# A graph layer with nearest neighbours: 48 quads of stage 1 multiplied as fp32r halves made by ScalarE and POOL

## The reference

```
z   = leaky_relu(lap(A, x) @ W1 + b1, 0.1)
S   = exp(-sqrt(|z_i - z_j|^2 + 1e-10) / 2), the 4 largest of each row kept
out = lap(S + A, x) @ W2 + b2
result = layernorm(x + out)
```

## Time and profile before

| | us |
|---|---|
| median of 3 runs | 2694.85 |
| lowest and highest run | 2694.80, 2696.83 |
| span of the profiled execution | 2759.5 |
| TensorE matmul busy in it | 2482.6 (90%) |
| DVE | 2319.8 (84%) |
| ScalarE | 1606.7 (58%) |
| POOL | 1195.4 (43%) |
| mean granted clock of TensorE | 0.969 |

### The profile page before, as it was taken

The page is one execution under the profiler, slowest core; times in us unless marked ns, Lnnn a source line. Parts: engine busy times, 40 slices in busy tenths (PEclk is TensorE's granted clock), DMA queues, the critical chain, the costliest instruction groups (busy, mean ns, idle before and its releaser), DMA issues.

```text
span 2759.5 us, 29107 instructions
## 1 busy us (share of the span) xinstructions
PE 2482.6 (90%) x9356; PEld 1722.4 (62%) x9356; DVE 2319.8 (84%) x1411; ACT 1606.7 (58%) x1905; POOL 1195.4 (43%) x987
## 2 busy tenths in 40 slices
PE   1367999999999998899999999999999987888978
PEld 0133444444677776578787877778787764666655
DVE  7998899977788888999999999999999773666766
ACT  0000000000477767999989899899988763555655
POOL 0000000000000000377778878788878956666760
PEclk9688999999999999999999999999999988999989
DMA  9999999995899960146555655555655688988975
GB/s 385 421 402 408 398 421 421 421 421 215 320 349 342 338 226 7 35 141 183 151 163 138 179 142 175 140 170 149 174 143 167 182 309 343 347 324 320 345 295 208
DMA packets 147949, 718.58 MB, mean 260 GB/s; under 512 B 19025, under 2 KB 26961, under 8 KB 86609
## 3 DMA queue, kind: packets, MB, share of 16 engines
q1 hardware_dynamic: 124384, 670.49, 65.6%
q0 software_dynamic: 18800, 37.77, 5.7%
q10 hardware_dynamic: 4608, 8.39, 0.8%
HBM read 680.40 MB, written 36.18 MB: 260 GB/s over the span
## 4 chain that ended last, share of the span: by engine, by line
PE 56%; issue 10%; ACT 10%; DVE 9%; DMA 7%; POOL 3%; another core or an unknown queue 3%; SPq 0%; ACTq 0%; POOLq 0%; DVEq 0%
PE PS L767 17%; PE PS L866 5%; PE PS L868 5%; PE PS L867 5%; DMA ring<-at 4%; ACT R L1141 3%; PE PS L834 3%; PE PS L910 3%; PE PS L921 3%; PE PS L911 3%; PE PS L830 2%; PE PS L831 2%; ACT ah_t L1191 2%; DVE R L1621 2%
## 5 line engine op out<-in xcount | busy, mean ns | idle before, releaser
L1299 POOL TENSOR_TENSOR al<-ring,ah 128x1024 fp32r<-128x1024 f32 x264 | 644.0, 2441 | 180.5 <-ACT ah L1112 168.7
L1621 DVE MAX8 R<-R 128x8 f32<-128x8192 f32 x64 | 555.9, 8685 | 68.1 <-ACT R L1141 67.9
L1141 ACT ACTIVATE R<-PS 128x1024 f32<-128x1024 f32 x512 | 518.1, 1018 | 114.1 <-PE PS L874 83.1
L1624 DVE FIND_INDEX8 R<-R,R 128x8 uint32<-128x8192 f32 x64 | 555.9, 8685 | 0.3 <-issue 0.3
L1272 POOL CAST zst<-zh 128x128 fp32r<-128x128 f32 (+1 forms) x64 | 26.2, 410 | 1113.2 <-DVE zl L1556 811.5
L866 PE MATMUL PS<-zh,zst 128*128 128x512 f32 x1024 | 407.3, 398 | 28.6 <-ACT PS L1127 12.7
L868 PE MATMUL PS<-zh,zst 128*128 128x512 f32 x1024 | 400.4, 391 | 0.0
L867 PE MATMUL PS<-zl,zst 128*128 128x512 f32 x1024 | 400.1, 391 | 0.0
L1456 POOL DMA_INDIRECT R<-xs_dram,R x256 | 279.7, 1093 | 145.2 <-issue 75.5
L1127 ACT ACTIVATE PS<-R 128x1024 f32<-128x1024 f32 x310 | 318.0, 1026 | 6.6
L1046 ACT ACTIVATE tiny<-rowsum 128x4 f32<-128x4 f32 x16 | 3.3, 205 | 481.2 <-DVE rowsum L1491 481.2
(11 more groups left out here) (177 smaller groups left out, 4469.9 us busy)
## 6 DMA issues: line engine op xcount, KB each, us to landing
R<-at SPq DMA_DIRECT2D x152, 1024.0 KB, 13.3
ring<-at SPq DMA_DIRECT2D x148, 1024.0 KB, 9.5
ring<-at SPq DMA_DIRECT2D x264, 512.0 KB, 3.9
cache<-at SPq DMA_DIRECT2D x117, 1024.0 KB, 20.2
raw_sq<-at SPq DMA_DIRECT2D x21, 1024.0 KB
raw_z<-at SPq DMA_DIRECT2D x20, 1024.0 KB
raw_ring<-at SPq DMA_DIRECT2D x20, 1024.0 KB
acc_dram<-R POOLq DMA_DIRECT2D x78, 256.0 KB, 5.7
```

The costliest lines, as they stand in the source:

```text
L1141: act.activation(score[j % 2][:, c * EC:(c + 1) * EC].rearrange("p (b c) -> p b c", b=2), pair(first, j, c), ACT.Copy).then_inc(copied, 1)
L1299: pool.tensor_tensor(al[:, k % SPLIT], raw[k % RAW], ah[:, k % SPLIT].bitcast(F32), ALU.subtract)\
L1621: v.max(top[:, j], score[j % 2]).then_inc(dve3, 1)
L1624: v.max_index(place[:, j], top[:, j], score[j % 2]).then_inc(placed, 1)
```

## The change

In row blocks 10 to 15 the eight quads with q < 8 are multiplied as halves: 48 quads. At the end of block 9 ScalarE makes the high halves of xs for q < 8 (two copies of 128x2048) and POOL the low ones. They lie in four slots of `cache`, which no load uses from load 144 on. Per halved quad ScalarE copies two pieces of 128x1024 to fp32r into one of two buffers, which lie over xs of q < 8; POOL subtracts each piece from the raw quad, with the result written over it, once DVE has added the quad; TensorE makes eight matmuls with the high part and four with the rest. Stage 2 writes its rests over the raw quads too, which frees two buffers for loads. In the order of loads and products of blocks 10 to 15 the halved quads are spread among the others.

```
-SLOTS_END = (0, 1, 2, 3, SLOTS_2, SLOTS_2 + B // TB)
+SLOTS_END = (0, 1, 2, 3, 4, 5)
+HALVED_FROM, HQ = 10, 8
+SLOTS_LOW = (SLOTS_2, SLOTS_2 + 1, SLOTS_2 + 4, SLOTS_2 + 5)
...
+def on_halves(b, q):
+    return b >= HALVED_FROM and q < HQ
...
+        if b == HALVED_FROM:
+            low = [HQ] + low[:HQ] + low[HQ + 1:]
+        elif b > HALVED_FROM:
+            low = spread(low[:HQ], low[HQ:-2]) + low[-2:]
...
-            k = next_slot(n, [*range(SLOTS_A), *(k for k, b in SLOTS_Y.items() if left(n) <= B * (b + 1)),
+            k = next_slot(n, [*(k for k in range(SLOTS_A) if n < (HALVED_FROM - 1) * B or k not in SLOTS_LOW),
+                              *(k for k, b in SLOTS_Y.items() if left(n) <= B * (b + 1)),
...
-            k = next_slot(n, [*range(SLOTS_B), *range(SLOTS_A, SLOTS_A + SLOTS_X)])
+            k = next_slot(n, [*range(SLOTS_2), *range(SLOTS_A, SLOTS_A + SLOTS_X)])
...
-        halves = range(min(q for r, q in two), B)
+        halves = range(HQ, B)
...
-                    sp.wait_ge(al_ok, m - n_one + 1)
+                    sp.wait_ge(prod2, m - n_one + 1)
...
+            def halved_product(b, q, first):
...
+                for k in range(TB):
+                    if k % PT == 0:
+                        pe.wait_ge(rnd_1, RESTS * m + k // PT + 1)
+                    pe.matmul(bank, half_of_xs(0, q)[:, k], ah_2[m % 2][:, k], start=first and k == 0, stop=False,
+                              skip_group_check=True)
+                    pe.matmul(bank, half_of_xs(1, q)[:, k], ah_2[m % 2][:, k], start=False, stop=False,
+                              skip_group_check=True)
+                for k in range(TB):
+                    if k % PT == 0:
+                        pe.wait_ge(al_1, RESTS * m + k // PT + 1)
+                    i = pe.matmul(bank, half_of_xs(0, q)[:, k], low[:, k], start=False, stop=False,
+                                  skip_group_check=True)
+                i.then_inc(prod1, 1)
...
+            def high_halves_low():
+                for k in range(2):
+                    tiles = slice(k * HQ * TB // 2, (k + 1) * HQ * TB // 2)
+                    act.wait_ge(xs_ok, (k + 1) * HQ // 2)
+                    free_of_stage_1(act, SLOTS_LOW[k])
+                    act.activation(xsh[:, tiles], xs[:, tiles], ACT.Copy).then_inc(xh_low, 1)
+
+            def round_1(m):
+                n = load_at[halved_1[m]]
+                act.wait_ge(ld_a[slot_of[n]], turn_of[n])
+                if m == 0:
+                    act.wait_ge(xl_low, 2)
+                wait_ah_free(act, m)
+                for part_ in range(RESTS):
+                    ks = slice(part_ * PT, (part_ + 1) * PT)
+                    act.activation(ah_2[m % 2][:, ks], slots_a[slot_of[n]][:, ks], ACT.Copy).then_inc(rnd_1, 1)
...
+            def root_of_rows(b):
+                if b:
+                    act.wait_ge(xs_ok, b)
                 act.wait_ge(sums_read, b + 1)
                 act.activation(tiny[:, 0, 0:TB], rowsum[:, b * TB:(b + 1) * TB], ACT.Sqrt).then_inc(root_ok, 1)
...
+            for b in range(B):
+                for i, q in enumerate(loads[b]):
+                    if b == B - 1 and i >= LOW_AT - 2:
+                        for h in halves[:-2]:
+                            if i == LOW_AT - 2 + (h - halves[0]) // 2:
+                                high_half(h)
+                    if (b, q) in half_at:
+                        round_1(half_at[b, q])
+                while saved < B and all(q < b for r, q in flat if r == saved):
+                    save_y(saved)
                     saved += 1
+                if b == HALVED_FROM - 1:
+                    high_halves_low()
+                root_of_rows(b)
...
+            def low_halves_low():
+                for k in range(2):
+                    tiles = slice(k * HQ * TB // 2, (k + 1) * HQ * TB // 2)
+                    pool.wait_ge(xh_low, k + 1)
+                    free_of_stage_1(pool, SLOTS_LOW[2 + k])
+                    pool.tensor_tensor(xsl[:, tiles], xs[:, tiles], xsh[:, tiles].bitcast(F32), ALU.subtract)\
+                        .then_inc(xl_low, 1)
+
+            def rest_1(m):
+                n = load_at[halved_1[m]]
+                quad = slots_a[slot_of[n]]
+                pool.wait_ge(rows_added, (B - 1) * (n // B) + max(n % B, 1))
+                for part_ in range(RESTS):
+                    ks = slice(part_ * PT, (part_ + 1) * PT)
+                    pool.wait_ge(rnd_1, RESTS * m + part_ + 1)
+                    pool.tensor_tensor(low_in[slot_of[n]][:, ks], quad[:, ks], ah_2[m % 2][:, ks].bitcast(F32),
+                                       ALU.subtract).then_inc(al_1, 1)
+
+            low_halves_low()
+            for m in range(len(halved_1)):
+                rest_1(m)
...
             def rest_2(n):
+                quad = slots_a[slot_of[n_one + n]]
                 v.wait_ge(rnd_2, n + 1)
-                if n < 2:
-                    v.wait_ge(prod1, max(prod_at[r, q] for r, q in flat if q // TB == n))
-                else:
-                    v.wait_ge(prod2, n - 1)
-                v.tensor_tensor(al_2[n % 2][:, :, :], slots_a[slot_of[n_one + n]], ah_2[n % 2][:, :, :].bitcast(F32),
+                v.tensor_tensor(low_in[slot_of[n_one + n]][:, :, :], quad, ah_2[n % 2][:, :, :].bitcast(F32),
                                 ALU.subtract).then_inc(al_ok, 1)
```

More of the change, by code:

```diff
@@ L83, in held, with spread @@
     return range(b - DEFER[b], b)
+def on_halves(b, q):
+    return b >= HALVED_FROM and q < HQ
+def spread(first, second):
+    n, m = len(first), len(second)
+    keyed = [((i + 0.5) / n, 0, q) for i, q in enumerate(first)] + [((i + 0.5) / m, 1, q) for i, q in enumerate(second)]
+    return [q for _, _, q in sorted(keyed)]
 def plan_ab():
@@ L156, in free_at @@
                 return n_one + SLOTS_B + 1
[L157 removed]
+            return left(now[k]) if now[k] < n_one else now[k] + 5
         return min((free_at(k), k) for k in may)[1]
@@ L223, in build @@
         slots_a += [R2[:, b * BC:b * BC + SLOT].rearrange("p (k c) -> p k c", c=BC) for b in SLOTS_Y.values()]
+        homes = [top_of["ring"] + k * SLOT * 4 for k in range(SLOTS_B)]
+        homes += [top_of["R1"] + (N + k * SLOT) * 4 for k in range(2)]
+        homes += [top_of["zh"] + k * SLOT * 4 for k in range(SLOTS_A - SLOTS_2)]
+        homes += [top_of["R1"] + k * SLOT * 4 for k in (2, 3)]
+        homes += [top_of["R2"] + b * BC * 4 for b in SLOTS_Y.values()]
+        low_in = [sb(f"low_in{k}", [P, TB, BC], F32R, at=a) for k, a in enumerate(homes)]
         total = R1[:, N + 2 * SLOT:N + 3 * SLOT]
@@ L444, in build @@
         ends = list(itertools.accumulate(sum(r == b for r, q in two) for b in blocks2))
-        halves = range(min(q for r, q in two), B)
+        halves = range(HQ, B)
+        halved_1 = [bq for bq in flat if on_halves(*bq)]
+        half_at = {bq: n for n, bq in enumerate(halved_1)}
+        low_done = max(prod_at[r, q] for r, q in flat if q < HQ and not on_halves(r, q))
         last_quad = {}
@@ L452, in build, with wait_ah_free @@
             made.append(max(e + 1, made[-1] + STEP_2 if made else 0))
-        assert max(prod_at[r, q] for r, q in flat if q < 2 * TB) <= prod_at[B - 1, 2 * TB - 1]
+        assert all(q >= HQ or r < HALVED_FROM for r, q in flat if not on_halves(r, q))
+        def wait_ah_free(eng, n):
+            if n < 2:
+                eng.wait_ge(prod1, low_done)
+            else:
+                eng.wait_ge(prod1, prod_at[halved_1[n - 2]])
         def free_of_stage_1(eng, k):
@@ L761, in product @@
                 started[b] += 1
+                if on_halves(b, q):
+                    halved_product(b, q, first)
+                    return
                 pe.wait_ge(ld_a[slot_of[n]], turn_of[n])
@@ L767, in product @@
                     i = pe.matmul(PS[:, b % YB], xs[:, q * TB + k], slots_a[slot_of[n]][:, k],
-                                  start=first and k == 0, stop=prod_at[b, q] == closed[b] and k == TB - 1)
+                                  start=first and k == 0, stop=prod_at[b, q] == closed[b] and k == TB - 1,
+                                  skip_group_check=True)
+                i.then_inc(prod1, 1)
+            def halved_product(b, q, first):
+                m = half_at[b, q]
+                bank, low = PS[:, b % YB], low_in[slot_of[load_at[b, q]]]
+                if m == 0:
+                    pe.wait_ge(xl_low, 2)
+                if first and b >= YB:
+                    pe.wait_ge(y_saved, b - YB + 1)
+                for k in range(TB):
[9 more added lines that the diff above has]
+                    i = pe.matmul(bank, half_of_xs(0, q)[:, k], low[:, k], start=False, stop=False,
+                                  skip_group_check=True)
                 i.then_inc(prod1, 1)
@@ L1064, in z_squares @@
+            round_2(0)
+            for q in halves[-2:]:
+                high_half(q)
+            round_2(1)
+            for b in range(saved, B):
```

(1 more changed line is left out.)

41 lines of the change are left out of this document (18 added, 23 removed).

## The result

The changed kernel takes 2878.66 us in the median of 4 runs (2875.3 to 2883.38), the kernel before 2694.82 beside it: ratio 1.0687, with the interval [1.0674, 1.0699]. The forecast was 2897 with a range of 2740 to 2970.

A forecast was written before the change was run, and what follows sets the result against it. TensorE was taken to set the pace, with DVE nearly as full. Blocks 10 to 14 +162, block 15 +30 and block 9 +9.4 gave +202 us on the median 2694.85: 2897 us, range 2740 to 2970.

The forecast's parts named there:

- POOL against DVE: Stage 1: POOL's differences and DVE's two-input adds take turns, so both queues add up within each block; blocks 10 to 14, +162.
- TensorE: 48 halved quads at 2.72 us for 3.44 take 34.6 us of work off TensorE, if halves come in time.
- ScalarE's gate: ScalarE's copies stand behind the square root, so a block's first half-quad is ready about 1.5 us after its start.
- Block time: Blocks 10 to 14 take 78 us each with POOL's and DVE's queues added: 390 against 227.6, +162.
- Block 9: POOL's two 128x2048 low-half differences, 9.6 us, fall in DVE's full block, which has 0.26 us to give: +9.4.
- Block 15: DVE's and POOL's work 78 us, then sums 0.95 and three products 10.3: 89.5 against 59.6, +30.
- The step on the last load: End of block 15: the last load has less cover before the column sums, 7.7 us open up; +6 without contention.
- Clock: A lower clock in half-loaded blocks lengthens the tail by up to 3 us a block, 15 in all; only in the range.
- A: Only POOL waits and starts when DVE falls idle: about 85 us a block, 2942 us; chance 0.2.
- B: POOL and DVE overlap in part: 50 to 75 us a block, 2735 to 2850 us; chance 0.13.
- C: No contention of long operations: +12.5 for blocks 10 to 14 and +6 for block 15, 2714 us; chance 0.13.
- D: Faster: POOL's piece is so short that TensorE sets the pace, point 4.4 us a quad; -27, 2668 us; chance 0.04.

The follow-up runs named there:

- Experiment 1: The changed kernel with DVE's two-input adds in blocks 10 to 15 replaced by one-input sums of the quad, running sum left out: 2746.09 us, 1.0195.
- experiment 4: The changed kernel with all stage 1 rests and the low halves of xs made by DVE, POOL idle, nothing left out: 2773.24 us, 1.0299.
- experiment 5: The changed kernel with ScalarE making the first two high halves of a block ahead of the square root: 2864.62 us, 1.0626.
- experiment 7: The changed kernel with TensorE's column sums of block 15 one product later: 2873.41 us, 1.0663.
- experiment 2: The changed kernel with POOL's stage 1 rests cut to 128x16 and TensorE taking the high half in their place: 2701.40 us, 1.003.
- experiment 3: The changed kernel with DVE's adds cut to 128x32 in blocks 10 to 15, the other row sums left out: 2731.19 us, 1.0142.

## Why the prediction was right

The step that carried it was **POOL against DVE**, where I took the whole cost in both directions between bounds of nothing and all. Experiment 1 removes the second operand, and most of the output with it, and 133 us go; experiment 4 removes POOL and 105 go, though DVE then does all the work. The adds of 4.33 beside pieces of 4.37 show the direction for which I had no row.

Point by point:

- *TensorE*, -34.6 us: the products did shrink, and it counted for nothing. TensorE was busy 262.1 us in the 375 of blocks 10 to 14. (That blocks 10 and 11 took 38.7 and 42.1 before was a rule of thumb: the reads give 39.7 and 41.0, with the same sum.)
- *ScalarE's gate*, halves ready at T + 1.5: POOL began at 516.90, T + 1.9. Right, and worth little (experiment 5).
- *Block time*, 78: measured 75.1. Block 11 is 1.9 + 60.8 of POOL + 9.8 of tail = 72.5. I had POOL's end near T + 68; it was T + 62.7. Written out, 1.5 for the start, 38.6 for POOL and 13 adds of 2.29 would even be T + 69.9. Two things were too large. Ten pieces stood in turns with adds and took 4.37 each, where a full 2.29 + 2.41 is 4.70: 3.3 us. And only those ten adds held POOL up, an eleventh made it wait 2.2 us for its quad, and the last two did their work after its last piece: 4.6 us. Instead, POOL's first six pieces ran at 2.5 us beside DVE's small operations, which I had not counted and which cost DVE some 10 us. The tail was 1.4 us longer than 8.4. So the adding of the two queues was right, and the order inside the block was not as I had it. The other four blocks, 74.4 to 77.7 us, were not taken apart in this way.
- *Block 9*, +9.4: +8.2. The two POOL differences of 128x2048 were 11.0 us together.
- *Block 15*, +30: +27.6. The sums came at T15 + 73.6, where I had 78, and 13.2 us later came stage 2, where it was 10.9 before. The step on the last load did not happen in this kernel: the 7.57 us before the sums were a wait for DVE's queue, and that they agree with the forecast's 7.7 is luck (experiment 7). Even in experiment 2, whose blocks are short and which lost just the +6 of that term, the last add waited only 0.20 us for its load: the sums came 2.6 us later than before, and 3.4 were lost behind them, with the clock at 0.76 after a wait of 6.6 us.
- *Clock*: left out of the sum, up to 15 us in the range. The windows show it at 0.75 in block 10 and 0.86 in block 14. In the tails, where it ends last, it cost about 1 us in block 11: a plain product took 4.50 and the next 3.60. Behind the sums of block 15 it cost the 2.3 us above, at a mean of 0.82.
- *At nothing*: the slots, stage 2 and the halves of xs cost nothing that shows; after 903.09 everything is 184 us later and no more.

**The rivals.** A (only POOL waits) is out: DVE's operations are stretched as well. B (partial) is what the 0.3 us a pair amounts to, some 3 us in block 11. C's mechanism is what experiment 3 leaves, and I had it too cheap: blocks 10 to 14 cost +22.8 instead of +12.5. In four of the five, POOL waits again for a high half after the block's start, 8.2 us in all, since there are only two buffers for them. D (faster) was further away than I said. Experiment 2 puts POOL's piece at 0.2 to 2.4 us, at or below the least piece of the earlier trace rows, and stays at 1.003. So the point of 4.4 us a quad from which TensorE would set the pace and win was wrong. D's full effect was -27, and experiment 2 has +7.5. Of the 34.5 us between them, 8.2 are block 9, which D put at nothing; 22 are blocks 10 to 14, 11.9 of waits for ScalarE and POOL and 10 of longer work, most of it clock; and 4 are block 15.

The Trainium skill (SBUF — State Buffer, "Who interferes with whom") says that a DVE instruction with two SBUF inputs contends with a GpSimd instruction that reads SBUF, that one with one input outside the two-port modes does not, that tensor_reduce never does on trn2, and that the loser stands still for the whole instruction. The trace agrees on the first (4.33 beside 4.37), on tensor_reduce (2.29 beside 2.35) and on copies by GpSimd as readers (3.09). It differs in the last by a little: the pair is some 0.3 us shorter than the sum of the two alone.

## What to carry to other kernels

Before work goes to an idle POOL, look at the operands of what DVE does in that stretch: if DVE's instructions have two inputs in SBUF and POOL reads SBUF, plan the two as one engine: here their pairs were only 7% shorter than the sum of the two, and the work cost less on the faster of them. Then add the queue of that one engine per beat (here 37.6 + 38.6 us against beats of 39.7 to 52.4) before counting what TensorE would save. Where the engine that would do the work has idle time in some beats alone, change only those: eight quads of 48 gave the only gain, and four more in a block whose DVE had no idle time at its end took it away again.

## What the hardware showed that I had not expected

- The pair of an add (2.29 alone) and a piece (2.35 to 2.41 alone) lasts 4.33 to 4.38 us; of an add and a copy (1.04 alone) 3.01 to 3.09. Both pairs are 0.25 to 0.35 us shorter than the two alone.
- Between POOL's pieces DVE's tiny operations on 128x4 took 2.12 to 2.31 us, also the one-input TENSOR_SCALAR (median 2187 ns); alone they take 0.16 to 0.17. RECIPROCAL did not wait (0.17 beside a piece in block 11), nor did the COPY from PSUM (0.16 beside a piece in experiment 5; in the changed kernel POOL is idle at that moment). In the other direction POOL's 128x16 pieces took from 0.21 up to 2.37 us behind an add. What differs between TENSOR_SCALAR and RECIPROCAL was not tried.
- In experiment 2 TensorE's clock was at its lower level (0.42 us a matmul for 0.23) for some 3 us after three waits of 1.6 to 1.9 us at a block's start, with some 95% of TensorE busy in the five blocks. After a fourth wait of 1.59 us it was not, and neither was it after the 1.91 us at the start of block 11 of the changed kernel, where the matmuls come every 0.23.
